# A routed-expert kernel: experts run in order of their counts, with 288, 288, 272, 272 and four times 256 columns

## The reference, cut to what matters

```python
probs_full = jax.nn.softmax(xt @ gate_w, axis=-1)
top_p, top_i = lax.top_k(probs_full, 2)
for k in range(2):
    e, w = top_i[:, k], top_p[:, k]
    pos = position of the token among those with the same expert, in token order
    keep = pos < 160                      # capacity per expert and per k
    buf[e, pos] = xt                      # kept tokens only
    h = gelu(buf @ w1 + b1)
    y = h @ w2 + b2 + gelu(buf @ wd) @ wu
    out += w * y[e, pos]                  # for kept tokens
sh = gelu(xt @ sw1 + sb1) @ sw2 + sb2 + gelu(xt @ swd) @ swu
result = x + out + 0.2 * sh
```

## Time and profile before

| | us |
|---|---|
| median of 3 runs | 205.91 (205.66 to 206.25) |
| the profiled execution | 205.94 |
| its span, first to last instruction | 204.0 |
| PE busy in the span | 193.3 (95%) |
| DVE, ACT, POOL busy | 141.6, 132.6, 110.7 |

### The profile page before, as it was taken

One profiled execution on the slowest core, in us unless ns is written; L12 is line 12 of the kernel. 1 busy time (PEld: TensorE's weight loads), 2 busy tenths in 40 slices (PEclk: granted clock), 3 DMA queues, 4 the chain that ended last, 5 costly groups with the idle time before them and its releaser, 6 DMA issues.

```text
span 204.0 us, 4078 instructions
## 1 busy us (share of the span) xinstructions
PE 193.3 (95%) x1489; PEld 186.0 (91%) x1489; DVE 141.6 (69%) x308; ACT 132.6 (65%) x282; POOL 110.7 (54%) x131
## 2 busy tenths in 40 slices
PE   6999999969999999999999999999999999999950
PEld 6996888968889999999999999999999999999940
DVE  4569599865584214777897878888888988988210
ACT  2337899901595109959959959959959959959000
POOL 5300012299373251412895898887886826817371
PEclk9999999999999999999999999999999999999997
DMA  5590663601928023145868977868769766702432
GB/s 176 152 330 19 205 222 74 213 3 48 287 71 267 0 66 103 29 140 180 195 119 263 199 174 222 179 163 261 146 176 261 133 205 198 114 3 23 46 38 33
DMA packets 23816, 29.24 MB, mean 143 GB/s; under 512 B 4442, under 2 KB 20564, under 8 KB 23796
## 3 DMA queue, kind: packets, MB, share of 16 engines
q1 hardware_dynamic: 19412, 23.03, 35.4%
q0 software_dynamic: 4016, 5.38, 16.9%
q10 hardware_dynamic: 368, 0.56, 0.8%
HBM read 23.92 MB, written 5.05 MB: 142 GB/s over the span
## 4 chain that ended last, share of the span: by engine, by line
PE 90%; DVE 3%; POOL 2%; POOLq 1%; issue 1%; ACT 1%
PE hid_ps L812 13%; PE hid_ps L814 13%; PE hid_ps L813 13%; PE y_ps L814 11%; PE y_ps L812 11%; PE y_ps L813 11%; PE y_ps L820 5%; PE turn_ps L977 3%; PE row_ps L993 1%; POOL out_rows L384 1%; POOLq L51 1%; PE y_ps L939 1%; PE hid_ps L833 1%; PE turn_ps L833 1%; PE y_ps L839 1%
## 5 line engine op out<-in xcount | busy, mean ns | idle before, releaser
L597 DVE TENSOR_TENSOR hid_l<-gelu_f,hid_h 128x320 fp32r<-128x320 f32 (+1 forms) x80 | 42.1, 535 | 20.1 <-ACT hid_h L504 17.8
L384 POOL DMA_INDIRECT out_rows<-y_row,slot_tok x24 | 43.9, 1828 | 17.1 <-DVE y_row L744 8.6
L503 ACT ACTIVATE gelu_f<-hid_ps,bias_t 128x320 f32<-128x320 f32 (+1 forms) x77 | 44.4, 577 | 6.0 <-PE hid_ps L814 4.9
L504 ACT ACTIVATE hid_h<-hid_ps,bias_t 128x320 fp32r<-128x320 f32 (+1 forms) x77 | 44.6, 579 | 0.0
L370 POOL DMA_INDIRECT slot_in<-slot_rows,slot_src x24 | 26.5, 1106 | 22.4 <-PE turn_ps L977 13.3
L812 PE MATMUL hid_ps<-xs_h,w_h 128*128 128x288 f32 x128 | 38.2, 298 | 0.0
L814 PE MATMUL hid_ps<-xs_h,w_l 128*128 128x288 f32 x128 | 37.7, 294 | 0.0
L813 PE MATMUL hid_ps<-xs_l,w_h 128*128 128x288 f32 x128 | 37.6, 294 | 0.0
L814 PE MATMUL y_ps<-hid_h,w_l 128*128 128x288 f32 x112 | 32.9, 294 | 0.0
L813 PE MATMUL y_ps<-hid_l,w_h 128*128 128x288 f32 x112 | 32.9, 294 | 0.0
L812 PE MATMUL y_ps<-hid_h,w_h 128*128 128x288 f32 x112 | 32.9, 294 | 0.0
(11 more groups left out here) (189 smaller groups left out, 407.8 us busy)
## 6 DMA issues: line engine op xcount, KB each, us to landing
w_raw<-in_L_ffn_w SPq DMA_DIRECT2D x16, 1024.0 KB
x_in<-in_x SPq DMA_DIRECT2D x2, 512.0 KB, 4.5
w_raw<-in_L_ffn_sw SPq DMA_DIRECT2D x1, 1024.0 KB
slot_rows<-token_row SPq DMA_DIRECT2D x2, 512.0 KB, 3.8
out_rows<-base SPq DMA_DIRECT2D x2, 512.0 KB, 3.2
wu_raw<-in_L_ffn_wu SPq DMA_DIRECT2D x24, 32.0 KB
w_raw<-in_L_ffn_sw ACTq DMA_DIRECT2D x1, 512.0 KB
w_raw<-in_L_ffn_sw SPq DMA_DIRECT2D x1, 512.0 KB, 5.3
```

Of the source, the lines that this page charges most:

```text
L384: pool.indirect_dma_start(out=out, out_offset=bass.IndirectOffsetOnAxis(ap=slot_tok[0:n, e, s:s + 1].bitcast(U32), axis=0), in_=y_row[0:n, ...
L503: act.activation(gelu_f[:, j % 3, 0:n], src[:, 0:n], ACT.Gelu, bias=bias(j - 1))
L504: act.activation(hid_h[:, j - 1, 0:n], src[:, 0:n], ACT.Gelu, bias=bias(j - 1)).then_inc(hid_gelu, 1)
L597: dve.tensor_tensor(hid_l[:, j - 1, 0:n], gelu_f[:, j % 3, 0:n], hid_h[:, j - 1, 0:n].bitcast(F32), ALU.subtract).then_inc(hid_split, 1)
```

## The change

The experts are run in falling order of their counts, and the sizes are fixed by rank: `SIZES` is 288, 288, 272, 272, 256, 256, 256, 256. The branch with these sizes is taken if each count fits: DVE adds 16 to the counts from rank 2 on and another 16 from rank 4 on, and compares the maximum with 288. Otherwise all experts run with 320 columns.

For this, PE counts after hidden tile 4 of half 0; ACT copies the raw counts out of PSUM behind its gelu of that tile; POOL ranks the experts in `rank_experts` (14 instructions, each waiting for the one before, then a copy into the integer tile `order`), placed before its `wd_hi_part(1,1)`. SP waits for `order` before it loads the first expert's weights, reads the expert's number for every rank into a register, and addresses the weights with it. DVE keys the tokens by rank instead of by expert and sorts the first-layer biases by rank (`sort_biases`). The keying moves behind the first shared output tile, the values behind the second, and DVE's four w1 chunks move behind later tiles. `turn_slots` makes only as many transposes as the next size needs (4 in place of 6 for 256 columns). `last_out` takes the third row tile first, and where the size is 256 that tile is one matmul instead of 25; the last scatters follow that order (tile 2, 0, 1). The warm-up is 7 times 16 matmuls instead of 9. The keys `keyed` lie in `y_t` now.

```diff
-WARM_UP = 9
+STEP = P // 8
+COUNT_AT = 4
+STEPS_AT = (2, 4)
+SIZES = [FEW - STEP * sum(r >= s for s in STEPS_AT) for r in range(E)]
+WARM_UP = 7
...
+        last_tiles = [ST - 1] + list(range(ST - 1))
...
@@ SP
             def load_first(v):
-                e = v - 1
+                if v == 1:
+                    sp.wait_ge(order_known, 1)
+                at_rank[v] = sp.value_load(order[0:1, v - 1:v], min_val=0, max_val=E - 1)
+                e = at_rank[v]
                 sp.wait_ge(w1_lo, v * CHUNKS)
...
-                sp.dma_start(w2_raw[:, :, :], w2_v[v - 1]).then_inc(w2_in, 16)
+                sp.dma_start(w2_raw[:, :, :], w2_v[at_rank[v]]).then_inc(w2_in, 16)
@@ POOL
+            def rank(ins):
+                ranks[0] += 1
+                ins.then_inc(ranking, 1)
+                pool.wait_ge(ranking, ranks[0])
+
+            def rank_experts():
+                pool.wait_ge(used_copied, 1)
+                pool.wait_ge(consts, 11)
+                rank(pool.tensor_scalar(count16[:, :, :], used_raw[:, :, :], float(CAP), float(E), ALU.min, ALU.mult))
+                rank(pool.tensor_tensor(tie[:, :], count16[:, 0, :], count16[:, 1, :], ALU.add))
+                rank(pool.tensor_tensor(tie[:, :], tie[:, :], col_of[:, 0, :], ALU.subtract))
+                rank(pool.tensor_tensor(is_more[:, :, :], tie[:, :].unsqueeze(1).to_broadcast([P, E, E]),
+                                        tie[:, :].unsqueeze(2).to_broadcast([P, E, E]), ALU.subtract))
+                rank(pool.tensor_scalar(is_more[:, :, :], is_more[:, :, :], 0.0, None, ALU.is_gt))
...
+                rank(pool.tensor_tensor(rank_at[:, :], is_more[:, :, 0], is_more[:, :, 1], ALU.add))
+                rank(pool.tensor_tensor(has_rank[:, :, :], rank_at[:, :].unsqueeze(1).to_broadcast([P, E, E]),
+                                        row_of[:, :, :], ALU.subtract))
...
+                pool.tensor_copy(order[:, :], tie[:, :]).then_inc(order_known, 1)
+                for i, s in enumerate(STEPS_AT):
+                    ins = pool.tensor_scalar(steps_down[:, i, :], rank_at[:, :], float(s), float(STEP), ALU.is_ge, ALU.mult)
+                ins.then_inc(rank_ready, 1)
+
+            rank_experts()
             wd_hi_part(1, 1)
             wu_hi_part(1, 1)
@@ ACT
                 gelu_tile(0, j, HALF, shared_bias)
+                if j == COUNT_AT:
+                    act.wait_ge(pos_made, 1)
+                    act.activation(used_raw[:, :, :], turn_ps[0][:, NT * K * E:(NT + 1) * K * E].rearrange(
+                        "p (k e) -> p k e", k=K), ACT.Copy).then_inc(used_copied, 1)
...
+            act.wait_ge(bias_sorted, 1)
@@ DVE
+            def key_tokens():
+
+                dve.wait_ge(rank_ready, 1)
+                step(dve.tensor_tensor(picked[:, :, :, :], chosen[:, :, :, :],
+                                       rank_at[:, :].unsqueeze(1).unsqueeze(1).to_broadcast([P, NT, K, E]), ALU.mult))
+                step(dve.tensor_reduce(rank_tok[:, :, :], picked[:, :, :, :], AX_X, ALU.add))
...
             for t in range(HTILES):
                 shared_row(t)
-                w1_chunk(t, 1, 1)
+                if t == 0:
+                    key_tokens()
+                if t == 1:
+                    value_tokens()
+                    w1_chunk(0, 1, 1)
+                if t == 2:
+                    w1_chunk(1, 1, 1)
+            w1_chunk(2, 1, 1)
+            w1_chunk(3, 1, 1)
...
             for t in range(HTILES, NT):
                 shared_row(t)
+                if t == HTILES:
+                    sort_biases()
@@ PE
+                tiles = [s for s in last_tiles if size > s * P]
+                if ST - 1 not in tiles:
+                    pe.matmul(last_bank[ST - 1][0:ST_ROWS[ST - 1], 0:D], low_s[:, (ST - 1) * P:SLOTS], wu_s[par][:, :],
+                              start=True, stop=True).then_inc(y_made, 1)
+                for s in tiles:
...
-                    if h == 0 and j == HT - 3:
+                    if h == 0 and j == COUNT_AT:
                         count_before()
...
-                        turn_slots(e + 1, other)
+                        turn_slots(e + 1, other, (sizes[e + 1] + P - 1) // P)
...
-                experts(FEW)
+                experts(SIZES)
             with pe.Else():
-                experts(SLOTS)
+                experts([SLOTS] * E)
```

More of the change, by code:

```diff
@@ L73, in build @@
         used_by = sb("used_by", [P, E])
+        count16 = sb("count16", [P, K, E])
+        tie = sb("tie", [P, E])
+        is_more = sb("is_more", [P, E, E])
+        rank_at = sb("rank_at", [P, E])
+        has_rank = sb("has_rank", [P, E, E])
+        order = sb("order", [P, E], I32)
+        row_of = sb("row_of", [P, E, E])
+        col_of = sb("col_of", [P, E, E])
+        steps_down = sb("steps_down", [P, 2, E])
+        rank_tok = sb("rank_tok", [P, NT, K])
+        bias_s = sb("bias_s", [P, E, NF])
         most_used = sb("most_used", [P, 1], I32)
+        used_raw = sb("used_raw", [P, K, E])
         place_number = sb("place_number", [P, P])
@@ L189, in build @@
         places_known = sem("places_known")
+        ranking = sem("ranking")
+        used_copied = sem("used_copied")
+        order_known = sem("order_known")
+        rank_ready = sem("rank_ready")
+        bias_picked = sem("bias_picked")
+        bias_sorted = sem("bias_sorted")
         keyed_made = sem("keyed_made")
@@ L379, in combine @@
                     pool.wait_ge(combined, e * (16 * ST))
-                for s in range(ST):
+                for i, s in enumerate(last_tiles if e == E - 1 else range(ST)):
                     n = ST_ROWS[s]
-                    if s > 0:
-                        pool.wait_ge(y_weighted, e * ST + s + 1)
+                    if i > 0:
+                        pool.wait_ge(y_weighted, e * ST + i + 1)
                     pool.indirect_dma_start(
@@ L653, in choose @@
                     step(dve.reciprocal(denom[:, :], denom[:, :]))
[L654 removed]
+                    dve.wait_ge(consts, 11)
                 else:
@@ L692, in place_tokens @@
                                          in1=slot_of[:, :, :], op0=ALU.mult, op1=ALU.add).then_inc(places_known, 1)
+            def key_tokens():
[3 more added lines that the diff above has]
+                step(dve.tensor_reduce(rank_tok[:, :, :], picked[:, :, :, :], AX_X, ALU.add))
+                step(dve.tensor_tensor(picked[:, :, :, :], rank_tok[:, :, :].unsqueeze(3).to_broadcast([P, NT, K, E]),
+                                       col_of[:, 0, :].unsqueeze(1).unsqueeze(1).to_broadcast([P, NT, K, E]), ALU.is_equal))
                 step(dve.tensor_tensor(in_tile[:, :, :, :], tile_of[:, :, :].unsqueeze(3).to_broadcast([P, NT, K, ST]),
@@ L705, in place_tokens, with sort_biases @@
                 step(dve.tensor_tensor(used_by[:, :], used[:, 0, :], used[:, 1, :], ALU.add))
+                for i in range(len(STEPS_AT)):
+                    step(dve.tensor_tensor(used_by[:, :], used_by[:, :], steps_down[:, i, :], ALU.add))
                 dve.tensor_reduce(most_used[:, :], used_by[:, :], AX_X, ALU.max).then_inc(used_known, 1)
+            def sort_biases():
+                picks = y_t[:, :, :].rearrange("p k n -> p (k n)")[:, 0:E * NF * E].rearrange("p (r f e) -> p r f e", r=E, f=NF)
+                dve.tensor_tensor(picks, bias_t[:, 0:N_BIAS1].rearrange("p (e f) -> p f e", e=E).unsqueeze(1).to_broadcast(
+                    [P, E, NF, E]), has_rank[:, :, :].unsqueeze(2).to_broadcast([P, E, NF, E]), ALU.mult).then_inc(bias_picked, 1)
+                dve.wait_ge(bias_picked, 1)
+                dve.tensor_reduce(bias_s[:, :, :], picks, AX_X, ALU.add).then_inc(bias_sorted, 1)
             def side_data():
@@ L750, in weigh_last @@
                 dve.wait_ge(slots_sided, 1)
-                for s in range(ST):
+                for i, s in enumerate(last_tiles):
                     n = ST_ROWS[s]
-                    dve.wait_ge(y_made, y_before(e + 2) + (s + 1))
+                    dve.wait_ge(y_made, y_before(e + 2) + (i + 1))
                     dve.tensor_scalar(y_row[0:n, s, :], last_bank[s][0:n, 0:D], slot_w[0:n, e, s:s + 1], None,
@@ L952, in last_out @@
                 pe.wait_ge(y_weighted, e * ST)
-                for s in range(ST):
+                pe.wait_ge(hid_split, hid_count(e + 2, 0))
+                tiles = [s for s in last_tiles if size > s * P]
[3 more added lines that the diff above has]
+                for s in tiles:
                     n = min(P, size - s * P)
@@ L975, in turn_slots @@
                 for k in range(KD):
-                    for s in range(ST):
+                    for s in range(tiles):
                         ins = pe.transpose(turn_ps[k][:, s * P:(s + 1) * P], slot_in[par][:, s, k * P:(k + 1) * P],
@@ L1022, in _, with experts @@
                     if h == 1 and t == 1:
-                        turn_slots(0, 0)
-            def experts(size):
-                for e in range(E):
```

(3 more changed lines are left out.)

30 lines of the change are left out of this document (21 added, 9 removed).

## The result

The changed kernel takes 213.56 us (median of 4 runs, 212.12 to 214.16), the kernel before in the same session 206.00 (4 runs, 205.66 to 206.25): a ratio of 1.037 [1.033, 1.040]. The forecast was 207.1 with a range up to 209.8. The direction was right, and the time is 3.8 us above the range. The profiled execution took 213.09 us, 7.15 more than that of before. Medians and ranges in this document are over all executions; two of ten in run 1 and two of four each in runs 4 and 5 ran over 1.5% above the fastest of their kernel, and without them these three medians are 203.13, 205.85 and 200.87 us.

A forecast was written before the change was run, and what follows sets the result against it. PE was taken as the bound, busy 193.3 of 204.0 us. 204.0 - 5.9 (sizes) + 0.6 (seam, last tile) + 4.1 (late matrices) + 2.35 (clock) = 205.15 span, 207.1 with 1.94 outside; range 202.3 to 209.8.

The forecast's parts named there:

- The start: Warm-up and first shared row: PE starts 1.5 us sooner, at 10.8; the 1.65 us stall goes; `map_slots` reached at 48.3.
- The chain in front of `map_slots`: Ranking, first expert's load and casts delay POOL's `at_place` to 44.7 to 57.1, making PE 4.1 us later.
- POOL's step of 0.47 us: Ranking on POOL: 14 steps and a copy at 0.47 us each, 7.1 us, so `order` is known at 37.1.
- The estimate of 0.14 us plus dispatch: POOL's ranking steps of 64 elements: by it the ranking lies near the lower end, the total near 204.5.
- The 0.7 us for SP: Between `order` and w1's transfer: SP wakes, reads the register and computes an address, taken from 0.1 to 1.5.
- The clock: PE's stall before `map_slots`: the granted clock falls and the restart costs 2.35 us, ends 0 and 2.4.
- The clock holds: Rival for PE's stall: some matmuls run there, so no clock price and 204.8 us; chance 0.2.
- What the sizes save: Experts on PE: fewer columns and slot transposes in ranks 2 to 7 save 5.9 us.
- one seam: Between experts 6 and 7: DVE's splits run late behind the shorter periods, putting 0.5 us on the last scatter.
- The experts give less: Rival: ACT or POOL becomes the bound at 13.6 us per expert, up to half of 3.7 us returned; 209; chance 0.1.
- The end: From the last `turn_results`, 21 to 22 us to the span's end as before; 0.6 us added for seam and last tile.
- the rival of unequal engines: Same as "The experts give less": ACT or POOL bounds the short expert periods; 209 us; chance 0.1.

The follow-up runs named there:

- run 1: Changed kernel with POOL making the 16 `at_place` matrices before the casts of the first expert's wd and wu; 203.61 us, ratio 0.989 to the kernel before.
- run 4: Changed kernel with the first expert's index fixed, so its weights load at the old time without waiting for the order; 207.51 us.
- run 5: Run 1 with ACT's and DVE's expert loops on the rank's own columns instead of 320; 202.72 us, ratio 0.988 to the kernel before.
- run 8: Run 1 with the warm-up back at 9 times 16 matmuls; 205.28 us, ratio 0.996 to the kernel before.
- run 2: Changed kernel with 140 extra unused matmuls just ahead of `map_slots`; 210.78 us, ratio 1.026 to the kernel before.
- run 3: Kernel before with the new sizes and `last_out` order alone, experts in old order, no ranking, tokens beyond each size left out; 205.24 us, ratio 0.997.
- run 7: Run 1 with the edits of both run 5 and run 6; 194.23 us, ratio 0.948 to the kernel before.
- run 9: Run 7 with 288 columns, so three row tiles, for every rank; 205.46 us, ratio 0.997 to the kernel before.
- run 6: Run 1 with POOL neither gathering nor scattering the third row tile for ranks 4 to 7; 199.34 us, ratio 0.973 to the kernel before.
- run 10: Run 7 with the casts of the first expert's wd and wu back ahead of `at_place`; 203.48 us, ratio 0.989 to the kernel before.

## Why the prediction was wrong

- **The start, right.** L937 (once L833) starts at 10.90, forecast 10.8; run 8 puts its worth at 1.4 to 1.7 us, forecast 1.5. PE reached `map_slots` at 48.14, forecast 48.3, so the stall at L918 is gone too.
- **The chain in front of `map_slots`, right within 1.5 us.** `order` 37.24 (37.1), `w1` issued at 38.40 (37.8), wd cast 43.96 (43.5), `at_place` 46.14 to 58.03 (44.7 to 57.1). POOL's step of 0.47 us was measured at 0.50. The estimate of 0.14 us plus dispatch, worked out from the 2048-element figure of GPSIMD Engine Reference (the Trainium skill, "Elementwise, side-by-side cycle accounting"), falls short here: the steps themselves last 0.19 to 0.89 us. The 0.7 us for SP had no row behind it; from the end of `order` to the issue of `w1` it took 0.97 (37.43 to 38.40). Of the 1.4 us by which `at_place` starts later than forecast, 0.5 were there at the wd cast, and the casts were slower than in quiet, 46.14 - 43.96 = 2.2 in place of 1.2; the prediction's upper end had 2.1.
- **The clock, right in its price.** Forecast 2.35; the trace gives 2.5 (12 matmuls in 5.28 us against 51.45 - 48.67 = 2.78 in the earlier trace rows) and run 2 gives 2.1 to 2.8. "The clock holds" falls. The clock was low for some 10 us, though, not for the 4 to 5 forecast; only the 5.3 us in which PE was dense cost time. That this stretch was about as long as the 4.7 us at the start, from which the price was taken, is luck.
- **What the sizes save, wrong; here the prediction failed.** The step took PE's removed matmul time, 5.9 us, as time removed from the span, less 0.5 at one seam. Run 3 gives 0.3 to 0.6 for the same cut, and in the changed kernel's own profile the periods and the end together give 0.46. The terms themselves were good: with the rest following, the periods give 5.1 (runs 7 and 9). What I read wrongly was the margin. The earlier trace rows show DVE at 12.84, ACT at 12.23, POOL at 11.87 of 15.03, and I concluded that each has over a microsecond left at 13.6. A mean over a period says nothing of the order in it: POOL's three scatters stand in one block of 7.4 us (135.62 to 143.03) in front of a cast that DVE waits for, and DVE reached 13.68 of 14.14. Runs 5 to 7 take those loads away and PE is full again. "The experts give less", with a chance of 0.1, had the mechanism but not its place: it counted up to half of 3.7 us, on top of which came the end.
- **The end, wrong.** Forecast -0.3: 0.9 less for PE's work behind the second mark, 0.6 more for the seam and the larger last tile (bounds 0 and 2). It took 2.8 us more than before, 3.1 above the forecast. Run 3 shows 2.0 of these with the sizes alone. DVE weighs expert 6's rows 11.4 us behind the transposes (188.63 - 177.25) and POOL's scatter then takes 3.65 in place of 2.84. The step treated that scatter as fixed by `turn_results`; it hangs on DVE, which is late. The later weighing (1.1), the longer issue (0.7) and the later landing (0.8) push the last expert's weighing, and three more scatters follow.
- **The sum.** 1.3 us from the front, 1.7 from the periods and 3.1 from the end are the miss of 6.15 in span. Had I given the rival of unequal engines the weight that the seams called for, the front alone (4.1 + 2.35, with 0 for the sizes) would have said 212.4.

Left open: whether DVE's subtractions are what makes a scatter's issue take up to 3.65 us, or only go with it; in which executions the clock falls when the matrices come first; and how run 7's gain over run 1 divides between its two edits, since run 5 varied by 4.5 us.

**The version to keep** is run 7: 194.23 us, 5.2% below the kernel before and 9% below the changed one. The ranking and the sizes pay once POOL makes the matrices first and ACT, DVE and POOL do only what the rank needs. The wide branch would need its own loops for them.

## What to carry to other kernels

Matmul columns removed from a PE-bound stage can be worth nothing, as here, until the engines that feed it shed their share too; read the margins not from mean busy time but from each seam where one engine's block of work stands ahead of what another waits for. When a load is made to depend on a computed index, look for the small instruction that stands behind that load on an in-order engine, and for everything that engine owes PE afterwards: here two casts, moved behind 16 matrices, were worth 10 us. A PE stall with a trickle of thin matmuls was paid twice here, once as the wait and once as the clock.

## What the hardware showed that I had not expected

- POOL's small dependent instructions cost 0.50 us each on the average, from one start to the next, 0.42 with 8 elements per partition and 0.65 with 64; single ones last 0.19 to 0.89 us.
- The granted clock fell while PE had a matmul of 72 columns every 0.6 us, and was still at 0.50 over the whole stretch 58.51:63.79, in which PE worked without a break. In run 10 it read 0.50 in 52:54 already, where the changed kernel had 0.91. In run 6, with the matrices first, it read 0.58 in 52:54 after PE had done the 16 thin matmuls from 48.17 to 51.34; in run 1, with theirs from 48.28 to 50.44, it stayed at 1.00. 140 useless matmuls in the stall took 2.1 to 2.8 us off the time.
- The same scatter instruction took from 1.43 to 3.65 us to issue. With next to none of DVE's subtractions beside it, it never took more than 1.56; all issues of 2.65 us and more had at least 1.45 us of them beside. Its place in the group of three does not decide: 189.90 is the first of its group, 139.47 the last.
